# One transfer of 128 rows with a leading dimension of four becomes four transfers of 32 rows

## The chip, the cores and the metric

The kernel runs on one core of a Trainium2 chip. The metric is device time in microseconds (us) of one execution. A core has five engines with their own instruction streams: PE (TensorE, matrix multiplication), DVE (VectorE), ACT (ScalarE), POOL (GpSimd) and SP (SyncE, which here only issues DMAs). 16 DMA engines move data between HBM and the on-chip memories, and are shared by everything that SP and ACT issue.

## The reference, cut to what matters

Two layers, float32 throughout. The first is a recurrent block over x of shape (B=16, L=128, E=512), with H=32 heads of S=16 channels. Its core:

```
r, k, v, w = four projections of a mix of neighbouring time steps, each (b, l, h, s)
def step(s, rkvw):
    r_t, k_t, v_t, w_t = rkvw
    a = k_t[..., :, None] * v_t[..., None, :]      # 16 x 16 for each batch and head
    out = einsum('bhi,bhij->bhj', r_t, u * a + s)
    s = a + w_t[..., :, None] * s
    return s, out
```

It is followed by a group norm, a gate g, a product with Wo, a residual, a layer norm and a feed-forward part with its own gate. The second layer is an attention over each batch of 128 channels by 512 positions against a context: two instance norms, 1x1 convolutions, a softmax of 512 x 512, and a residual.

## The kernel before, in words

The 16 batches are cut into four quarters q of four batches. For each quarter a front computes the projections (streams `a` and `p`) and writes k, v, w, r, g to scratch tensors in HBM (`scr_k` and so on). v is written twice, once of it as `scr_vs`, whose rows are one head of one batch: 16 channels by 128 times, 2,048 floats, 8 KB. Then each batch `bb` goes through the recurrence (stream `scan`), its normalisation (`end`), later the rest of the first layer (`c`, by quarter) and the attention (`l`, `l1`, `l2`, `l3`, by batch). On every engine the instructions of these streams stand in one order that is written out by hand (`ORDER_PE`, `ORDER_POOL`, `ORDER_SP` and so on, lines 32 to 133), as counts of steps of each stream. An engine that waits in one step runs nothing that stands behind it.

The recurrence of a batch has four steps m, one per channel group of the key side. All 128 partitions are used: partition = (channel of k within the group, head), so that every head stands four times, once in each group of 32 partitions. k, w and r come as 128 rows (tiles `KR`, `WG`). v, however, is needed in full by each of the four partition groups: the tile `VB[:, 2 + s]` (s = bb % 2, two buffers) holds the same 32 rows of v four times. It comes with one DMA for each batch, line 499, whose source is the 32 rows with a leading dimension of four and step zero.

For each step POOL computes three products or sums of 128 x 1008 (lines 696, 700, 704) from `KR`, `WG` and this tile. The first of a batch waits on `d_vb` (line 692). DVE runs two scans over their result (line 1150) and multiplies it by r (line 1029), PE sums over the channels (line 1440, semaphore `p_scan`). The products of step k use `VB[:, k % 2]`, so line 696 of step k waits also for PE's line 1440 of step k - 2.

All loads and a part of the stores stand in SP's order. Per batch, stream `load` issues k (484), w (491), v (499), r (505) and then v in the plain layout over the rows of r (510). Each waits for its buffer to be free: the v load of batch bb for POOL's products of batch bb - 2 and for the `scr_vs` stores of the quarter. Between them stand the loads and stores of other streams: `scr_g` stores (422), the copies `LT<-LE` of 32 partitions of the front (453), x (418, 537), the `scr_o` store of the recurrence's result (516), `scr_g` and `scr_o` loads (525, 529), and the context and the output (548, 563). ACT issues the stores of k, v, w and r (786, 788, 831).

Of the kernel before, what the change touches and what calls it, by code (L numbers as in the profile page):

```python
# [6 lines left out]
B, L, E = 16, 128, 512  # L7
NQ = 4
QB = B // NQ
NT = QB * L  # L10
C4 = E // P
H, S = 32, 16
# [236 lines left out]
def rwkv_attention_kernel(nc, x, ctx, w8, w1, w2, td1, td2, wl1, vecs, st01, s0, u, out):  # L249
    with ExitStack() as es:  # L250
        def sb(name, shape):
            return es.enter_context(nc.sbuf_tensor(name, shape, F32))

        def sem(name):
            return es.enter_context(nc.semaphore(name))
# [23 lines left out]
        VB = sb("VB", [P, 4, 2, S, N2])  # L279
# [31 lines left out]
        vs_rows = dr_vs[0:B * H * S * L].rearrange("(q h b n) -> q b h n", q=NQ, h=H, b=QB)  # L311
# [8 lines left out]
        d_vb = [sem(f"d_vb{i}") for i in range(2)]  # L320
# [76 lines left out]
        def stored(n, q):  # L397
            return [(d_st_[n][m], 16 * (q + 1)) for m in range(4)]
# [9 lines left out]
        def of_batch(n, bb):  # L408
            return dr[n][bb // QB].rearrange("c p (b t) -> b p c t", b=QB)[bb % QB]


        def sync_program(sp):
            w = Waits(sp)
# [57 lines left out]
            def stream_load():  # L471
                sp.dma_start(S0[:], s0).then_inc(d_s0, 16)
                yield
                w.wait_ge(d_vec, 32)
                sp.dma_start(dr_vs[0:1].unsqueeze(0), VEC[0:1, 0:1]).then_inc(d_s0, 16)
                yield
                for bb in range(B):
                    q, s = bb // QB, bb % 2
                    for ready in stored("k", q):
                        w.wait_ge(*ready)  # L480
                    if bb >= 2:
                        w.wait_ge(g_kv, 12 * (bb - 1))
                        w.wait_ge(v_kr2, 3 * (bb - 1))
                    sp.dma_start(KR[:, s, 0], of_batch("k", bb)).then_inc(d_kg[s], 16)
                    yield
                    for ready in stored("w", q):
                        w.wait_ge(*ready)
                    if bb >= 2:
                        w.wait_ge(g_kv, 12 * (bb - 1))
                        w.wait_ge(v_kr2, 3 * (bb - 1))  # L490
                    sp.dma_start(WG[:, s], of_batch("w", bb)).then_inc(d_wg[s], 16)
                    yield
                    if bb >= 2:
                        w.wait_ge(g_kv, 12 * (bb - 1))
                    for c in range(C4):
                        w.wait_ge(d_vs[c], 64 * (q + 1))
                    w.wait_ge(d_s0, 32)
                    src = vs_rows[q, bb % QB].unsqueeze(0).to_broadcast([4, H, S * L])
                    sp.dma_start(VB[:, 2 + s].rearrange("p s j n -> p (s j n)"), src).then_inc(d_vb[s], 16)
                    yield  # L500
                    for ready in stored("r", q):
                        w.wait_ge(*ready)
                    if bb >= 2:
                        w.wait_ge(p_end, 3 * bb - 4)
                    sp.dma_start(KR[:, s, 1], of_batch("r", bb)).then_inc(d_rg[s], 16)
                    yield
                    for ready in stored("v", q):
                        w.wait_ge(*ready)
                    w.wait_ge(a_rg, bb + 1)
                    sp.dma_start(KR[:, s, 1], of_batch("v", bb)).then_inc(d_v4, 16)  # L510
                    yield
# [28 lines left out]
            def stream_l(ln):  # L540
# [29 lines left out]
                if ln == 0:  # L570
                    for cs in range(4):
                        w.wait_ge(d_out[cs], 32 * sum(place(bb)[0] == cs for bb in range(B)))
                    yield

            weave(ORDER_SP, {"a": stream_a(), "p": stream_p(), "w": stream_w(), "x": stream_x(), "load": stream_load(), "end": stream_end(), "c": stream_c(),
                             **{n: stream_l(i) for i, n in enumerate(LANES)}})


        def pool_program(po):
            w = Waits(po)  # L580
# [91 lines left out]
            def stream_scan():  # L672
                for k in range(C4 * B):
                    bb, m = divmod(k, C4)
                    bv = VB[:, k % NB]
                    s = bb % 2
                    KO, KE = KR[:, s, 0, m, ODD], WG[:, s, m, ODD]
                    if m == 0:

                        w.wait_ge(d_wg[s], 16 * (bb // 2 + 1))  # L680
                        w.wait_ge(g_id, 3)
                        if bb >= 2:
                            w.wait_ge(a_wr, 4 * (bb - 1))
                        po.tensor_tensor(WP[:, s, :, 1:N2], WG[:, s, :, 0:N2 - 1], WG[:, s, :, N2:L - 1],
                                         ALU.mult).then_inc(g_wp, 1)
                        yield
                        w.wait_ge(d_kg[s], 16 * (bb // 2 + 1))
                        w.wait_ge(g_wp, 2 * bb + 1)
                        po.tensor_tensor(WG[:, s, :, ODD], WG[:, s, :, ODD], KR[:, s, 0, :, EVEN],
                                         ALU.mult).then_inc(g_wp, 1)  # L690
                        yield
                    w.wait_ge(d_vb[s], 16 * (bb // 2 + 1))
                    if k >= NB:
                        w.wait_ge(p_scan, k - NB + 1)
                    vo, ve = bv[:, 0, :, 1:N2], bv[:, 1, :, 1:N2]
                    po.tensor_tensor(vo, KO[:, 0:N2 - 1].unsqueeze(1).to_broadcast([P, S, N2 - 1]),  # L696
                                     VB[:, 2 + s, 0, :, 1:N2], ALU.mult).then_inc(g_kv, 1)
                    yield
                    w.wait_ge(g_wp, 2 * (bb + 1))
                    po.tensor_tensor(ve, KE[:, 0:N2 - 1].unsqueeze(1).to_broadcast([P, S, N2 - 1]),  # L700
                                     VB[:, 2 + s, 1, :, 1:N2], ALU.mult).then_inc(g_kv, 1)
                    yield
                    w.wait_ge(g_kv, 3 * k + 2)
                    po.tensor_tensor(vo, vo, ve, ALU.add).then_inc(g_kv, 1)  # L704
                    yield
# [23 lines left out]
            def stream_l(ln):  # L729
                for k in range(len(BATCHES[ln])):  # L730
                    w.wait_ge(af[ln], 5 * k)
                    yield from mean_rstd(3 + ln, 2, gl_[ln], 4 * k, vf[ln], 4 * (k + 1))

            weave(ORDER_POOL, {"a": stream_a(), "scan": stream_scan(), "end": stream_end(), "c": stream_c(),
                               **{n: stream_l(i) for i, n in enumerate(LANES)}})

# [904 lines left out]
```

## Time and profile before

| | |
|---|---|
| median of 3 runs | 1060.73 us (1055.62 to 1067.09) |
| the profiled execution's own time | 1064.16 us |
| its span in the trace | 1062.4 us |
| PE / DVE / POOL / ACT busy | 85% / 65% / 51% / 37% of the span |
| mean granted TensorE clock | 0.921 |
| DMA | 100.33 MB, mean 94 GB/s |

"Busy" is time with an instruction at work. Idle time is put down to what released the engine at its end. The chain is followed back from the last instruction, at each step to what released it. For a DMA the time from its issue to its landing is given, so it holds the waiting in the DMA queue too.

### The profile page before, as it was taken

Reading aid. Unit: us, or ns where it says so; the run is one execution under the profiler, and the core shown is the slowest. Engines: PE = TensorE matmul, PEld = TensorE weight load, DVE = VectorE, ACT = ScalarE, POOL = GpSimd, SP = SyncE. Lnnn points to the kernel's source line nnn. Section 1 sums busy time; section 2 is a strip of 40 time slices with the busy share of each in tenths; the row PEclk is TensorE's granted clock in tenths of the full one; section 3 lists DMA queues with packets and bytes.
Section 4 is the critical chain, followed back from the end, with each engine's and each line's share of the span. In section 5 each row is a group of like instructions: output and inputs, shape, how many; then the busy total and the mean of one; then the engine's idle time right before and its main releaser. Section 6 shows DMA issues by size and latency. Waiting matters only on the chain.

```text
span 1062.4 us, 10584 instructions
## 1 busy us (share of the span) xinstructions
PE 907.6 (85%) x3588; PEld 400.7 (38%) x3588; DVE 690.3 (65%) x907; ACT 388.9 (37%) x755; POOL 538.6 (51%) x573
## 2 busy tenths in 40 slices
PE   1789969995989958899769988789793999999998
PEld 1234423341334313334324434334341444444454
DVE  5235377764899848899846899569686744362341
ACT  2112212231144112222323544434342354576195
POOL 2000274443769868799658689678677421010100
PEclk9788989898899969699989999899895899999999
DMA  7152455333563535453451322333230123010101
GB/s 258 30 139 73 136 158 119 119 90 99 108 176 123 129 109 121 157 169 105 109 174 37 90 60 64 103 111 98 72 78 22 31 72 116 1 40 1 40 1 39
DMA packets 92983, 100.33 MB, mean 94 GB/s; under 512 B 21890, under 2 KB 63106, under 8 KB 90882
## 3 DMA queue, kind: packets, MB, share of 16 engines
q1 hardware_dynamic: 66306, 78.69, 25.7%
q10 hardware_dynamic: 26624, 20.98, 7.5%
q8 instruction: 28, 0.46, 0.2%
q14 instruction: 25, 0.20, 0.1%
HBM read 65.05 MB, written 33.55 MB: 93 GB/s over the span
## 4 chain that ended last, share of the span: by engine, by line
PE 46%; DMA 22%; POOL 11%; DVE 9%; issue 4%; ACT 4%; ACTq 3%; SPq 2%; POOLq 0%; DVEq 0%
PE PS L1318 30%; DMA VB<-scr_vs 14%; DMA scr_g<-STG 4%; PE PS L1543 3%; POOL VB L704 3%; POOL VB L696 3%; POOL VB L700 3%; PE PS L1325 3%; PE PS L1440 2%; PE PS L1381 2%; ACTq L786 2%; PE PS L1520 2%; DMA KR<-scr_r 2%; DVE VB L1029 2%; DVE VB L1150 1%
## 5 line engine op out<-in xcount | busy, mean ns | idle before, releaser
L1318 PE MATMUL PS<-M,W 128*128 128x512 f32 x672 | 338.4, 646 | 36.8 <-DVE STG L1032 16.6
L696 POOL TENSOR_TENSOR VB<-KR,VB 128x1008 f32<-128x1008 f32 x64 | 127.8, 1997 | 173.2 <-DMA VB<-scr_vs 95.2
L1318 PEld LDWEIGHTS PS<-M,W 128*128 128x128 f32 x672 | 129.8, 205 | 212.0 <-issue 162.6
L1150 DVE TENSOR_TENSOR_SCAN VB<-PS,VB 128x512 f32<-128x512 f32 x128 | 149.2, 1207 | 52.8 <-POOL VB L704 48.5
L704 POOL TENSOR_TENSOR VB<-VB 128x1008 f32<-128x1008 f32 x64 | 151.5, 2367 | 3.5
L1029 DVE TENSOR_TENSOR VB<-VB,PS 128x2048 f32<-128x2048 f32 x64 | 146.0, 2282 | 1.3
L700 POOL TENSOR_TENSOR VB<-WG,VB 128x1008 f32<-128x1008 f32 x64 | 129.2, 2018 | 0.2
L1032 DVE SCALAR_TENSOR_TENSOR PS<-PS,VEC,SX 128x512 f32<-128x512 f32 x80 | 60.2, 753 | 90.9 <-PE PS L1381 81.7
L586 POOL TENSOR_SCALAR NM<-MV 128x2 f32<-128x2 f32 (+1 forms) x24 | 6.6, 273 | 221.9 <-DVE MV L1278 130.0
L1318 PE MATMUL PS<-W,M 128*128 128x512 f32 x224 | 108.4, 610 | 0.0
L1440 PE MATMUL PS<-VB,HEAD 128*32 128x512 f32 x512 | 72.3, 639 | 19.8 <-DVE VB L1029 11.1
L778 ACT ACTIVATE STG<-PS 128x512 f32<-128x512 f32 x48 | 28.5, 594 | 136.9 <-PE PS L1318 117.1
L1296 DVE TENSOR_REDUCE SM<-PS 128x1 f32<-128x512 f32 x64 | 43.8, 688 | 42.3 <-PE PS L1543 42.0
L1381 PE MATMUL PS<-LE,W 32*128 32x512 f32 x64 | 43.1, 758 | 30.0 <-DVE M L1029 11.1
L1318 PE MATMUL PS<-W,SX 128*128 128x512 f32 x128 | 61.2, 597 | 0.0
L1543 PE MATMUL PS<-LS 128*128 128x512 f32 x112 | 60.3, 636 | 0.0
L1318 PEld LDWEIGHTS PS<-W,M 128*128 128x128 f32 x224 | 41.4, 195 | 45.7 <-issue 44.7
L1029 DVE TENSOR_TENSOR M<-PS,EXT 128x512 f32<-128x512 f32 x80 | 55.1, 689 | 2.1
L852 ACT ACTIVATE PS<-WP 128x512 f32<-128x512 f32 x64 | 38.2, 598 | 42.3 <-DVE VB L1150 35.5
L1520 PE MATMUL PS<-LS,WL 128*128 128x512 f32 x56 | 32.6, 679 | 20.1 <-ACT LS L937 15.2
L972 ACT ACTIVATE LE<-PS,SM 128x512 f32<-128x512 f32 x44 | 30.0, 683 | 51.4 <-DVE SM L1296 51.2
L1032 DVE SCALAR_TENSOR_TENSOR STG<-STG,PS 128x512 f32<-128x512 f32 x32 | 21.6, 680 | 36.9 <-ACT STG L776 18.3
(166 smaller groups left out, 1267.7 us busy)
## 6 DMA issues: line engine op xcount, KB each, us to landing
VB<-scr_vs SPq DMA_DIRECT2D x16, 1024.0 KB
W<-in_w SPq DMA_DIRECT2D x8, 1024.0 KB, 9.5
scr_vs<-STG ACTq DMA_DIRECT2D x64, 64.0 KB, 4.2
scr_v<-STG ACTq DMA_DIRECT2D x16, 256.0 KB, 5.2
scr_w<-STG ACTq DMA_DIRECT2D x16, 256.0 KB, 2.0
scr_k<-STG ACTq DMA_DIRECT2D x16, 256.0 KB, 2.0
KR<-scr_k SPq DMA_DIRECT2D x16, 256.0 KB, 4.9
WG<-scr_w SPq DMA_DIRECT2D x16, 256.0 KB, 5.4
```

What stands on the lines that cost most here:

```text
L696: po.tensor_tensor(vo, KO[:, 0:N2 - 1].unsqueeze(1).to_broadcast([P, S, N2 - 1]), VB[:, 2 + s, 0, :, 1:N2], ALU.mult).then_inc(g_kv, 1)
L700: po.tensor_tensor(ve, KE[:, 0:N2 - 1].unsqueeze(1).to_broadcast([P, S, N2 - 1]), VB[:, 2 + s, 1, :, 1:N2], ALU.mult).then_inc(g_kv, 1)
L704: po.tensor_tensor(vo, vo, ve, ALU.add).then_inc(g_kv, 1)
L1029: return dv.tensor_tensor(o, a, b, op)
L1032: return dv.scalar_tensor_tensor(out=o, in0=a, scalar=s, in1=b, op0=op0, op1=op1)
L1150: sc = dv.tensor_tensor_scan(s_, PS[:, 5, :], b_, 0.0, ALU.mult, ALU.add)
L1296: dv.reduce_max(SM[:, cs, tc, 0:1], PS[:, BANK_L[bb, ("sc", tc)], :], AX_X, negate=True).then_inc(vb[ln], 1)
L1318: mm = pe.matmul(o, l, r, start=i == 0, stop=i == 3)
L1381: mm = pe.matmul(PS[:, ns[i], :], W2[DM * g:DM * g + DM, 2 * i + j, :], low_rank(f, i), start=True, stop=True)
L1440: mm = pe.matmul(PS[32 * g:32 * g + 32, 4, :], HEAD[:, m, 0], VB[:, k % NB, :, 4 * g:4 * g + 4].rearrange("p s j n -> p j s n"), start=m = ...
L1520: pe.matmul(PS[:, n, :], WL[:, j, :], X[:, j, :], start=True, stop=True).then_inc(pf[ln], 1)
L1543: pe.matmul(PS[:, n, :], X[:, 2, tc * P:(tc + 1) * P], X[:, 3, :], start=True, stop=True).then_inc(pb[ln], 1)
```

## The change

The one DMA becomes a loop over the four partition groups, each with a source of 32 rows and no broadcast, all on the same queue and semaphore. The semaphore then rises by 64 for each batch, and POOL's wait is scaled to that. Nothing else changes.

```
-                    src = vs_rows[q, bb % QB].unsqueeze(0).to_broadcast([4, H, S * L])
-                    sp.dma_start(VB[:, 2 + s].rearrange("p s j n -> p (s j n)"), src).then_inc(d_vb[s], 16)
+
+                    for c in range(4):
+                        sp.dma_start(VB[H * c:H * c + H, 2 + s].rearrange("p s j n -> p (s j n)"),
+                                     vs_rows[q, bb % QB]).then_inc(d_vb[s], 16)
                     yield
...
-                    w.wait_ge(d_vb[s], 16 * (bb // 2 + 1))
+                    w.wait_ge(d_vb[s], 64 * (bb // 2 + 1))
```

## Rows read from the trace of the kernel before

**Rows 1.** The page: engines over the span, and the granted clock in 40 slices.
```profile
PE 907.6 (85%) x3588; PEld 400.7 (38%) x3588; DVE 690.3 (65%) x907; ACT 388.9 (37%) x755; POOL 538.6 (51%) x573
...
PEclk9788989898899969699989999899895899999999
```
**Rows 2.** The page: the chain that ended last, by line.
```profile
PE PS L1318 30%; DMA VB<-scr_vs 14%; DMA scr_g<-STG 4%; PE PS L1543 3%; POOL VB L704 3%; POOL VB L696 3%; POOL VB L700 3%; PE PS L1325 3%; PE PS L1440 2%; PE PS L1381 2%; ACTq L786 2%; PE PS L1520 2%; DMA KR<-scr_r 2%; DVE VB L1029 2%; DVE VB L1150 1%
```
**Rows 3.** The chain in time: start us, us, what.
```profile
105.31 23.67 DMA VB<-scr_vs
...
147.60 20.18 DMA scr_g<-STG
...
227.84 19.11 DMA KR<-scr_r
...
654.26 19.05 DMA VB<-scr_vs
```
**Rows 4.** DMA issues: KB of each, median us from issue to landing.
```profile
KR<-scr_k SPq DMA_DIRECT2D x16, 256.0 KB, 4.9
...
KR<-scr_r SPq DMA_DIRECT2D x16, 256.0 KB, 12.7
...
XN<-scr_g SPq DMA_DIRECT2D x4, 1024.0 KB, 5.8
...
LT<-LE SPq DMA_DIRECT2D x16, 64.0 KB, 2.0
```
**Rows 5.** Line 453 (`LT<-LE`): landing, least, median and most.
```profile
DMA to landing us min/median/max: 2.0/2.0/20.0
```
**Rows 6.** Stretches: length, busy us of each engine, clock, DMA share, GB/s.
```profile
110.00:112.00 2.00, 2.00 (x12) 1.21 (x10) 0.00 (x0) 0.79 (x2) 0.11 (x1) 1.00 0.93 357
668.00:672.00 4.00, 2.86 (x12) 0.71 (x9) 0.00 (x0) 0.00 (x0) 0.00 (x0) 1.00 0.24 73
784.00:788.00 4.00, 4.00 (x10) 1.44 (x8) 3.66 (x8) 1.15 (x4) 3.78 (x4) 1.00 0.28 70
```
**Rows 7.** Who waited for whom: us in total, times, longest.
```profile
POOL VB L696 <- DMA VB<-scr_vs: 95.2, 8, 22.3
```
**Rows 8.** POOL in time: three of those eight waits, idle us in brackets.
```profile
129.05 2.00 POOL L696 TENSOR_TENSOR VB<-KR,VB 128x1008 f32<-128x1008 f32 x1 [18.95 <-DMA VB<-scr_vs]
...
246.29 2.00 POOL L696 TENSOR_TENSOR VB<-KR,VB 128x1008 f32<-128x1008 f32 x1 [22.28 <-DMA VB<-scr_vs]
...
539.95 2.00 POOL L696 TENSOR_TENSOR VB<-KR,VB 128x1008 f32<-128x1008 f32 x1 [14.18 <-DMA VB<-scr_vs]
```
**Rows 9.** PE in time: idle us before the instruction in brackets.
```profile
248.86 2.07 PE L1318 MATMUL PS<-M,W 128*128 128x512 f32 x2 [9.71 <-DVE STG L1032]
...
380.90 1.19 PE L1381 MATMUL PS<-LE,W 32*128 32x512 f32 x1 [10.04 <-issue]
```
**Rows 10.** Stretches as in rows 6: a load awaited, the middle, the end.
```profile
105.00:129.00 24.00, 24.00 (x74) 11.70 (x74) 9.73 (x12) 8.54 (x14) 1.60 (x3) 1.00 0.49 153
...
100.00:860.00 760.00, 648.28 (x2754) 277.27 (x2753) 573.97 (x684) 252.60 (x497) 513.98 (x494) 0.91 0.37 105
860.00:1062.40 202.40, 194.97 (x658) 95.55 (x658) 75.76 (x161) 116.53 (x225) 16.69 (x51) 1.00 0.14 41
```
**Rows 11.** Seven stretches behind late loads: last one, and the sum.
```profile
796.00:825.00 29.00, 9.41 (x48) 3.61 (x47) 17.67 (x18) 8.09 (x15) 21.75 (x24) 0.56 0.07 22
sum 182.00, PE 112.36 PEld 46.13 DVE 108.17 ACT 43.50 POOL 113.96; mean PE 16.05 PEld 6.59 DVE 15.45 ACT 6.21 POOL 16.28
```
**Rows 12.** Seven stretches with no late load: second one, and the sum.
```profile
300.00:358.00 58.00, 56.37 (x276) 24.07 (x274) 56.11 (x68) 21.80 (x42) 48.56 (x52) 1.00 0.44 141
...
sum 264.00, PE 244.36 PEld 106.08 DVE 236.19 ACT 105.15 POOL 213.79; mean PE 34.91 PEld 15.15 DVE 33.74 ACT 15.02 POOL 30.54
```
**Rows 13.** SP's issues: line 499 (ns min/median/max), and one of line 422.
```profile
L499 SPq DMA_DIRECT2D VB<-scr_vs x16: 524/582/651, 105.3 to 780.5; - x16
...
363.01 12.91 SPq L422 DMA_DIRECT2D scr_g<-STG  x1
```

## The prediction

> **What bounds the kernel now.** I read the page first. PE is busy 85% of the span and no other engine comes near, but its clock digits fall below 9 in many slices [rows 1]: PE is interrupted, and what interrupts it is what a change can win. Then the chain: after the main matmul line its largest piece is the v load, `VB<-scr_vs`, with 14% (some 149 us) [rows 2]. In order of time it stands there in single pieces of about 20 us, the first of them and a later one shown at 23.67 and 19.05 us, and between them other transfers that take equally long, `scr_g` 20.18 and `KR<-scr_r` 19.11 us [rows 3]. A load of 1 MB need not take that long: `XN<-scr_g`, the same size in 128 rows, lands in 5.8 us [rows 4].
>
> The table of DMA issues shows who else pays. `KR<-scr_k` and `KR<-scr_r` move the same 256 KB into the same tile. The first is issued ahead of the v load and lands in 4.9 us, the second is issued right behind it and lands in 12.7 [rows 4]. `LT<-LE` lands in 2.0 us as a rule and in 20.0 at worst [rows 5].
>
> The windows say why. In 668 to 672 us, when little but the v load is under way, the mean busy share of the 16 DMA engines is 0.24 and 73 GB/s are moved; at 784 to 788 it is 0.28 and 70. With 128-row transfers at work it is 0.93 and 357 GB/s [rows 6]. 0.24 x 16 = 3.8: the v load looks like the work of four engines, and everything queued behind it waits for those four. The source's leading dimension is four. By the Trainium skill (DMA: Bandwidth & Descriptors, section "Why a DMA increments its semaphore by 16 and not by 1") a DMA uses at most as many engines as divide its outermost dimension on both sides, so four here and 16 for 32 rows; the share of 0.24 to 0.28 agrees.
>
> **The load, costed.** An engine at work on it moves 73 / 3.8 = 19 GB/s. 16 of them would move 304, so 1,048,576 bytes take 3.4 us. To that I add the landing of a small transfer of 32 partitions, 2.0 us [rows 4], and three more issues of 0.58 us on SP [rows 13] before the last part is even started, 1.7. The sum is 7.1 us against 19.05 [rows 3], **12.0 us less for each load**. The trace has no 256 KB transfer into 32 partitions, so bounds: below, 5.8 us, the same bytes in 128 rows; above, four times the 4.9 us of a 256 KB load one after another plus 1.7, 21.3 us [rows 4, 13]. I take 7.1, since 73 GB/s is this very load's own rate.
>
> A rule of the Trainium skill speaks against splitting by partitions. SBUF — State Buffer (section "Door 1: The DMA port swizzle") says that 32 partitions reach half of the memory's 16 ports, with an asymptote of about 218 GB/s. By that figure 1 MB would take an estimated 4.8 us in place of my 3.4, and the load 8.5; no row here shows a transfer of this shape at size.
>
> **What POOL gains.** It waited for the v load eight times, 95.2 us in all, 22.3 at most [rows 7]. The three waits above 12 us (18.95, 22.28, 14.18) [rows 8] can give back 12.0 each: 95.2 - 6.95 - 10.28 - 2.18 = 75.8 us. That is a cap, because PE must have nothing else to do: while the first load was awaited PE was busy 24.00 of 24.00 us [rows 10], and that work stays.
>
> **What reaches the end.** The last 202.4 us have PE busy for 194.97 at full clock [rows 10], and the first 100 us hold no v load. I leave both as they are and work on the 760 us between, of which PE is idle 760 - 648.3 = 111.7 us [rows 10]. I read PE's own idle times there. Two come straight from the queue behind the load: 10.04 us before line 1381, which wants an `LT<-LE` issued behind the v load of 358 us, and 9.71 us before line 1318, where DVE was held by ACT, and ACT by `KR<-scr_r` [rows 9]. The others follow as late products. They lie in seven stretches (129 to 147, 227 to 247, 358 to 390, 518 to 554, 673 to 694, 754 to 780, 796 to 825 us), 182 us with PE busy for 112.36 [rows 11]: 69.6 of the 111.7 us of idle. Seven stretches without a late load (200 to 227, 300 to 358, 413 to 466, 466 to 489, 580 to 604, 604 to 654, 705 to 734) have 264 us with 244.36 busy, 92.6% [rows 12].
>
> - *Idle.* If the 182 us ran as the others do, they would take 112.36 / 0.926 = 121 us: **61 us less**. It is below POOL's cap of 75.8, as it must be.
> - *Clock.* PE's granted clock fell to 0.56 over 796 to 825 us, in which it was busy 9.41 of 29 us [rows 11], and the middle has a mean of 0.91 against 1.00 at the end [rows 10]. Were the mean to rise to 0.95, the 648.3 us would shrink by 648.3 x (1 - 0.91/0.95) = 27 us. Not all matmuls are on the path: I take half, **14 us**, with bounds 0 and 27.
> - *SP.* Three more issues of 0.582 us for each of 16 batches are 27.9 us on its queue [rows 13]. Queued behind them are r (line 505), the `scr_g` stores and `LT<-LE`; behind those wait ACT (line 859), ACT's copies into STG and PE (line 1381). About half of the loads are awaited by someone, and of what follows less: I charge a third, **9 us** lost, with bounds 0 and 28. One `scr_g` issue was itself held 12.91 us behind a v load [rows 13]; that goes, and I count nothing for it.
> - *The wait.* 64 in place of 16 per batch costs nothing; POOL waits for the last of four.
>
> Sum: 61 + 14 - 9 = 66 us. The profiled execution took 1064.2 us, so 998 on its own scale. It stands 3.4 us above the median of the runs, so **about 995 us**, say 996.
>
> **The rivals.**
> - *The written order keeps most of it.* The order on each engine was fixed with loads of 20 us in it. PE may meet the scan steps no earlier, and only the direct waits vanish: 9.71 + 10.04 [rows 9] = 20 us, 1044 and so 1041. For it: PE's 24.00 of 24.00 us. Against it: PE and DVE ran at 97% each over 300 to 358 us, where loads were on time [rows 12].
> - *PE alone is left.* The middle runs as densely as the end, 194.97 / 202.4 = 96.3%: 648.3 / 0.963 = 673, 87 us less, with the whole clock term 114, less SP's 9: 105 us, so 1064 - 105 - 3 = 956. Against it: DVE is busy 574 of the 760 us [rows 10], and would be at 87% of 655.
> - *No effect.* The four parts run one after another and together take what the one took, plus SP's 9 us: 1061 to 1070. For it is only that the bytes are the same. The Trainium skill has a rule of this kind (DMA: Bandwidth & Descriptors, "Rules for kernel authors": two transfers to disjoint partition halves serialise, use one over 128 partitions). The share of 0.24 [rows 6] speaks against: the engines were mostly unused.
> - *Slower.* A part of 256 KB into 32 partitions lands like `KR<-scr_k`, in 4.9 us, and the parts do not overlap. The load becomes 21.3 us, 2.3 more at each of the eight awaited ones, 18 us, and SP's 9: 1064 + 27 - 3 = 1088. It decides from a part of (19.05 - 1.7) / 4 = 4.3 us on. Against it: 64 KB into 32 partitions land in 2.0 us [rows 4].
>
> **How the numbers follow.** Forecast 0.60 (its own range 965 to 1025, which holds the bounds of the clock and of SP's issues), PE alone 0.13, written order 0.17, no effect 0.05, slower 0.05. Measurement can tell about 1% of this kernel, 1050 to 1071. Faster by over 1%: 0.60 + 0.13 + nearly all of 0.17, 0.89. Within 1%: 0.06. Slower: 0.05. The range 950 to 1043 takes in both neighbours of the forecast and leaves out the tails of each, no effect and slower, under 0.2 together.
>
> **What would show it.** Right: the v parts land within about 7 us of the first issue; `VB<-scr_vs` leaves the chain or falls under 3%; POOL's 95 us of waiting for it fall under 25; `KR<-scr_r` lands near the 4.9 us of `KR<-scr_k`; the most of `LT<-LE` falls from 20.0 towards 5; the DMA share is near 0.9 for short whiles with no plateau at 0.25; PE busy falls by some 14 us through the clock. Wrong: parts over 4 us each, a DMA share that stays at a quarter, or POOL's line 696 waiting for PE's line 1440 as long as it had waited for the load.

## The result and the profile after

The changed kernel takes 991.95 us (988.33 to 997.10, 4 runs) against 1061.2 us (1055.62 to 1067.09, 4 runs) before: a ratio of 0.935, with a 95% interval of 0.928 to 0.942. The forecast was 996 us in a range of 950 to 1043. The profiled executions have spans of 1062.4 and 989.1 us.

The page of the changed kernel, with the engines and the granted clock [rows 1], and the chain that ended last, by engine and by line [rows 2]. The load is now line 500; lines behind it are two higher than before.
```profile
PE 899.4 (91%) x3588; PEld 398.1 (40%) x3588; DVE 691.0 (70%) x907; ACT 389.1 (39%) x755; POOL 540.4 (55%) x573
...
PEclk9797999799879979699999999999998999999999
...
PE 56%; POOL 23%; DVE 9%; issue 5%; ACT 3%; ACTq 2%; DMA 1%; SPq 0%; POOLq 0%; DVEq 0%
PE PS L1320 37%; POOL VB L706 6%; POOL VB L698 5%; POOL VB L702 5%; PE PS L1383 4%; PE PS L1545 3%; PE PS L1327 3%; PE PS L1442 3%; ACTq L788 2%; PE PS L1522 2%; DVE M L1034 2%; DVE PS L1034 2%; DVE M L1031 2%; PE PS L1456 1%; DVE VB L1031 1%
```
`VB<-scr_vs` has left the chain; all DMAs together hold 1% of it. In its place stand PE and POOL's products.

DMA issues of the changed kernel [rows 4], and the landing of line 453, `LT<-LE` [rows 5]:
```profile
VB<-scr_vs SPq DMA_DIRECT2D x64, 256.0 KB, 7.0
...
KR<-scr_k SPq DMA_DIRECT2D x16, 256.0 KB, 4.3
...
KR<-scr_r SPq DMA_DIRECT2D x16, 256.0 KB, 5.7
```
```profile
DMA to landing us min/median/max: 1.9/2.0/4.9
```
`KR<-scr_r`, still issued right behind the v load, lands in 5.7 us where it had taken 12.7, and the worst `LT<-LE` in 4.9 where it was 20.0: the queue behind the load moves.

Who waited for whom [rows 7], and SP and POOL around the load of batch 2 [rows 8]:
```profile
POOL VB L698 <- PE PS L1442: 78.1, 21, 10.6
...
POOL VB L698 <- DMA VB<-scr_vs: 22.3, 3, 11.2
```
```profile
218.26 2.08 SPq L500 DMA_DIRECT2D VB<-scr_vs  x4
```
```profile
226.23 2.00 POOL L698 TENSOR_TENSOR VB<-KR,VB 128x1008 f32<-128x1008 f32 x1 [11.19 <-DMA VB<-scr_vs]
```
From the first issue to POOL's start are 8.0 us, and POOL's waits for v fell from 95.2 to 22.3 us. Its waits for PE's line 1440 (now 1442) did not grow in their place. In the kernel before they were already
```profile
POOL VB L696 <- PE PS L1440: 77.9, 23, 11.6
```

Stretches of the changed kernel: one in which the v load has the DMA engines to itself [rows 6], then the middle and the end [rows 10].
```profile
112.00:114.00 2.00, 2.00 (x10) 1.11 (x9) 0.00 (x0) 1.71 (x3) 0.00 (x0) 1.00 1.05 216
```
```profile
100.00:786.70 686.70, 639.71 (x2755) 275.11 (x2754) 574.81 (x684) 252.87 (x497) 516.27 (x495) 0.94 0.43 116
786.70:989.10 202.40, 194.86 (x658) 95.44 (x657) 75.60 (x161) 116.52 (x225) 16.64 (x51) 1.00 0.15 41
```
The whole time saved lies in the middle: 760 us became 686.7, the end kept its 202.4. PE's idle there (the stretch less PE's busy time) fell from 111.7 to 47.0 us, and its busy time from 648.3 to 639.7, at a mean clock of 0.94 in place of 0.91.

### The profile page after: what moved, and what is told of

It reads as the page before. It is cut to its first block, busy times and chain, and to the rows that moved or that the text cites. A ratio compares the mean times of both kernels' runs of the same rounds, so it can differ in the third digit from the quotient of the medians.

```text
span 989.1 us, 10632 instructions
## 1 busy us (share of the span) xinstructions
PE 899.4 (91%) x3588; PEld 398.1 (40%) x3588; DVE 691.0 (70%) x907; ACT 389.1 (39%) x755; POOL 540.4 (55%) x573
## 4 chain that ended last, share of the span: by engine, by line
PE 56%; POOL 23%; DVE 9%; issue 5%; ACT 3%; ACTq 2%; DMA 1%; SPq 0%; POOLq 0%; DVEq 0%
PE PS L1320 37%; POOL VB L706 6%; POOL VB L698 5%; POOL VB L702 5%; PE PS L1383 4%; PE PS L1545 3%; PE PS L1327 3%; PE PS L1442 3%; ACTq L788 2%; PE PS L1522 2%; DVE M L1034 2%; DVE PS L1034 2%; DVE M L1031 2%; PE PS L1456 1%; DVE VB L1031 1%
## 5 line engine op out<-in xcount | busy, mean ns | idle before, releaser
L1320 PE MATMUL PS<-M,W 128*128 128x512 f32 x672 | 333.2, 638 | 20.6 <-DVE M L1034 12.6
L1320 PEld LDWEIGHTS PS<-M,W 128*128 128x128 f32 x672 | 127.7, 202 | 193.5 <-issue 160.6
L698 POOL TENSOR_TENSOR VB<-KR,VB 128x1008 f32<-128x1008 f32 x64 | 128.4, 2006 | 100.5 <-PE PS L1442 78.1
L1320 PE MATMUL PS<-W,M 128*128 128x512 f32 x224 | 105.6, 596 | 0.0
L1383 PE MATMUL PS<-LE,W 32*128 32x512 f32 x64 | 45.8, 803 | 20.3 <-DVE M L1031 11.3
L1034 DVE SCALAR_TENSOR_TENSOR LS<-PS,WOB,X 128x512 f32<-128x512 f32 x14 | 10.5, 748 | 52.6 <-PE PS L1320 52.6
L1383 PE MATMUL PS<-LT,W 32*128 32x512 f32 x64 | 46.2, 809 | 0.0
```

What stands on the lines that cost most here:

```text
L1034: return dv.scalar_tensor_tensor(out=o, in0=a, scalar=s, in1=b, op0=op0, op1=op1)
L1320: mm = pe.matmul(o, l, r, start=i == 0, stop=i == 3)
L1383: mm = pe.matmul(PS[:, ns[i], :], W2[DM * g:DM * g + DM, 2 * i + j, :], low_rank(f, i), start=True, stop=True)
```

## The experiments

Ratios are to the kernel before on the same chip, with 95% intervals; where the total of one run is set against that of another, the two may come from different chips, and the ratios are the safer comparison. Diffs are against the changed kernel unless it says otherwise, and are cut to the lines that matter (`...`); where the number of transfers changes, POOL's wait is scaled to it.

**The changed kernel again** (no edit), the base of the later runs.

> The changed kernel once more, on the same chip as the next three, as their base. 988 to 997 us, 0.93 to 0.94 of the kernel before.

990.04 us, ratio 0.935 (0.931 to 0.938).

### What sets the pace of the load

**Two transfers of 64 rows.**
```
+                    for c in range(2):
+                        sp.dma_start(VB[64 * c:64 * c + 64, 2 + s]...,
+                                     vs_rows[q, bb % QB].unsqueeze(0).to_broadcast([2, H, S * L]))...
```


> Two transfers of 64 rows, each with a leading dimension of two and step zero. Theory A (the leading dimension sets how many DMA engines work on a transfer): two engines, DMA share near 0.13 while it runs alone, about 20 to 32 us of data time for each load, slower than the kernel before: 1080 to 1180 us. Theory B (it is only that one transfer is cut into parts that overlap): between before and after, 1000 to 1050 us.

1172.6 us, ratio 1.107 (1.102 to 1.112). A stretch in which little but the load runs, and POOL's wait:
```profile
121.00:125.00 4.00, 4.00 (x10) 1.71 (x9) 1.35 (x2) 0.60 (x1) 0.00 (x0) 1.00 0.13 50
```
```profile
POOL VB L698 <- DMA VB<-scr_vs: 192.9, 12, 31.4
```
The share of 0.13 is two of 16 engines, as it was four in [rows 6]. So it is the leading dimension, not the number of parts, that sets how many engines work. A split in two, with a leading dimension of two, makes the kernel 11% slower. Theory A is shown. The pace of one engine is not fixed, though: 50 GB/s over two engines are 25 each, where four had 73 / 3.8 = 19 each. No run shows why.

**One transfer of 128 rows without the leading dimension.** It reads the quarter's 128 rows one after another, so nearly all partitions, in all four groups, get other rows than they should. The source is then one contiguous megabyte, where it had been 32 rows that lie 32 KB apart, read four times. The bytes, the row of 8 KB and the number of rows written are the same.
```
(against the kernel before)
+        vs_all = dr_vs[0:B * H * S * L].rearrange("(q r n) -> q r n", q=NQ, r=P)
+                    sp.dma_start(VB[:, 2 + s]..., vs_all[q]).then_inc(d_vb[s], 16)
```


> One transfer of 128 rows without the leading dimension: it reads the quarter's 128 rows of 8 KB, so the three later partition groups get other rows than they should; as many bytes, one issue. Theory A (leading dimension): all 16 DMA engines, over 300 GB/s, data time 3 to 3.5 us, landing about 6 us after the issue, total 984 to 992 us, no slower than the change. Theory B (the number of rows or bytes of a single transfer is what made it slow): about 16 us of data time and 1050 to 1065 us.

998.43 us, ratio 0.943 (0.938 to 0.948). The load:
```profile
110.00:113.00 3.00, 3.00 (x17) 1.97 (x16) 0.00 (x0) 1.90 (x3) 0.00 (x1) 1.00 1.04 422
```
The load moves at 422 GB/s on all engines, over the 300 that theory A named, so number of rows and bytes had never been the trouble. Its landing was 8.0 us after the issue in the median, not about 6. Its total missed theory A's range by 6 us, on the slow side, which is taken up below.

**Eight transfers of 16 rows**, run twice.
```
+                    for c in range(8):
+                        sp.dma_start(VB[16 * c:16 * c + 16, 2 + s]...,
+                                     vs_rows[q, bb % QB][16 * (c % 2):16 * (c % 2) + 16])...
```


> Eight transfers of 16 rows in place of four of 32. Theory A (the pace of a part is set by how many memory ports its partitions reach, 217 GB/s for 32 rows, so half of it for 16): DMA share near 1 but only about 110 GB/s while the v load runs alone, the eight parts take about 10 us of data time against 5.2, first POOL waits about 5 us longer each, total 1000 to 1012 us. Theory B (the DMA engines were the only limit, 16 rows still use all 16): data time stays near 5 us plus four more issues, total 990 to 998 us.

> The eight transfers of 16 rows once more, now on one chip with the changed kernel. Its load takes longer (7.9 against 5.8 us of data) and it yet took 984 us beside 992. Theory A (a real difference, from where PE's idle time and so its clock falls): 6 to 10 us below the changed kernel again, PE busy about 887 against 899 us. Theory B (the chip or chance): within 3 us of it.

984.19 us, ratio 0.931 (0.927 to 0.934), and 986.10 us, ratio 0.932 (0.928 to 0.936). The pace:
```profile
144.00:148.00 4.00, 2.53 (x8) 0.98 (x8) 1.98 (x4) 0.00 (x0) 4.00 (x3) 1.00 1.07 143
222.00:224.00 2.00, 2.00 (x16) 1.74 (x15) 2.00 (x2) 0.00 (x0) 0.00 (x0) 1.00 0.99 152
```
With all engines busy in all three, the load moves 422 GB/s into 128 partitions, 216 in parts of 32 and 143 to 152 in parts of 16. So the pace goes down with the partitions that a part covers, as theory A said, though 143 is above the 110 it named. The size of a part goes down with them, and the 422 also had a contiguous source, so these runs do not separate the three. Size alone does not hold a part of 256 KB to 216 GB/s: in the changed kernel, while the loads of k and w run (256 KB each, 128 partitions), more is moved:
```profile
106.00:107.00 1.00, 1.00 (x9) 0.64 (x6) 0.84 (x2) 1.00 (x3) 0.00 (x0) 1.00 1.13 339
```
The total, however, lies below both theories' ranges: the slower load gave the same or a slightly better time. The second time it was 4 us under the changed kernel with PE busy 891.9 against 896.3 us, between the two theories. No cost of the four further issues on SP for each batch shows either. Against the changed kernel on one chip (0.935, 0.931 to 0.938) the intervals overlap, so a gain of eight parts over four is not shown.

### Which part of the gain is which

**v early, but the queue blocked.** Behind the four parts goes a transfer with the old source into a scratch tensor, so this kernel also moves 1 MB more per batch.
```
+                    w.wait_ge(d_dum, 16 * bb)
+                    sp.dma_start(dum, vs_rows[q, bb % QB].unsqueeze(0).to_broadcast([4, H, S * L]))...
```


> The changed kernel, and behind the four parts of each load a further transfer with the old source and its leading dimension of four, into a scratch tensor in HBM that nobody reads: v is early, but the queue behind it is held as before. Theory A (most of the gain is v's own arrival at POOL): 1000 to 1020 us, KR<-scr_r landing at 10 to 13 us again. Theory B (most of it is the queue behind the load): 1040 to 1065 us.

1030.59 us, ratio 0.973 (0.968 to 0.978). POOL's waits for v are 22.0 us, as in the changed kernel. The slow landing of `KR<-scr_r` is back, and about half of PE's wait of 10.04 us for `LT<-LE` [rows 9]:
```profile
KR<-scr_r SPq DMA_DIRECT2D x16, 256.0 KB, 13.5
```
```profile
372.93 1.19 PE L1388 MATMUL PS<-LE,W 32*128 32x512 f32 x1 [5.46 <-issue]
```
Neither theory's range held it; it lies between them. The blocked queue costs at most 1030.6 - 992 = 39 us with v on time; at most, because the added traffic is in it.

**v late, but the queue free.** POOL does idle work ahead of the first product of the eight batches that had waited.
```
+                    if m == 0:
+                        for _ in range(DELAY.get(bb, 0)):      # {0: 23, 2: 25, 5: 26, 9: 26, ...}, 163 in all
+                            w.wait_ge(g_dum, len(done_))
+                            (po.memset(DUM[:], 0.0) if not done_ else
+                             po.tensor_tensor(DUM[:], DUM[:], DUM[:], ALU.mult)).then_inc(g_dum, 1)
...
```


> The changed kernel with idle work on POOL (163 small products of 128 x 128, about 73 us together) ahead of the first product of the eight batches whose load POOL had waited for before: v is late for POOL again, but the DMA queue is free. Theory A (v's arrival and the blocked queue each carry a part of the gain that adds up with the 28 us which the opposite experiment left): 1020 to 1035 us. Theory B (the queue is all that mattered): 990 to 1005 us.

1059.04 us, ratio 1.002 (0.999 to 1.005). The idle work on POOL, the landing of r behind the load, and POOL's first product of batch 2:
```profile
L703 POOL TENSOR_TENSOR DUM<-DUM 128x128 f32<-128x128 f32 x162 | 68.9, 425 | 25.7 <-DMA VB<-scr_vs 13.5
```
```profile
KR<-scr_r SPq DMA_DIRECT2D x16, 256.0 KB, 4.1
```
```profile
248.11 2.00 POOL L708 TENSOR_TENSOR VB<-KR,VB 128x1008 f32<-128x1008 f32 x1
```
All of the gain is gone, with the queue free (`KR<-scr_r` lands in 4.1 us). The idle work stands behind what is left of the wait for v (13.5 us, and 8.1 before the memset), so it holds POOL for 68.9 + 21.6 = 90.5 us, against 95.2 of waits before. That product starts at 248.11 us where it had started at 246.29 [rows 8]: v is as late as it was. DVE's busy time, 688.8 us against 691.0 in the changed kernel, shows no cost of the idle work to DVE.

Both theories fall, and with them the thought that the two causes add up. Against the kernel before, freeing the queue while v stays late brings nothing (1059 us), v early behind a queue still blocked brings 28 (1031), and both together bring 69 (992). They lie on the same stretches. The delay stands in place of the waits only roughly, and this is the limit of the reading.

**The slow load, issued sooner.** The kernel before with two steps of SP's order moved.
```
(against the kernel before, in ORDER_SP)
-    ... load:2 x:1 load:2 a:1 load:1 ...          load:2 end:1 load:2 a:3 ...
+    ... load:3 x:1 load:1 a:1 load:1 ...          load:3 end:1 load:1 a:3 ...
```


> The kernel before, one transfer with the leading dimension of four, with the two steps of SP's order moved (v of batch 0 ahead of x, v of batch 2 ahead of the scr_o store). Theory A (a slow load can be partly hidden by issuing it sooner): POOL's 22.3 us wait in batch 2 goes, 1035 to 1052 us. Theory B (what stands behind the load pays for it): within 1% of the kernel before.

1043.83 us, ratio 0.987 (0.982 to 0.992). POOL's wait:
```profile
POOL VB L697 <- DMA VB<-scr_vs: 70.9, 7, 16.6
```
As theory A had it: the 22.3 us wait of batch 2 is gone, and a fifth of the gain could be had without touching the transfer.

### What a still earlier load brings

**The same order in the changed kernel.**
```
-    ... load:2 x:1 load:2 ...      load:2 end:1 load:2 a:3 ...
+    ... load:3 x:1 load:1 ...      load:3 end:1 load:1 a:3 ...
```

> The changed kernel with two steps of SP's order moved: the v load of batch 0 ahead of the x load, and that of batch 2 ahead of the scr_o store which it stood behind. Theory A (what is left of POOL's wait for v is SP's order, 8.7 and 11.2 of its 22.3 us): that wait falls from 22.3 to under 10 us, and the total by 5 to 12 us against the changed kernel. Theory B (PE or DVE carry the path there): the wait falls and the total stays within 3 us.

994.46 us, ratio 0.939 (0.935 to 0.943). POOL's waits for v fell as expected, to 5.3 us, 4.0 of them in batch 0, and the total did not:
```profile
114.67 2.00 POOL L699 TENSOR_TENSOR VB<-KR,VB 128x1008 f32<-128x1008 f32 x1 [4.00 <-DMA VB<-scr_vs]
```
```profile
POOL VB L699 <- PE PS L1443: 95.7, 22, 18.3
```
Part of the wait turned into one for PE: 95.7 us where it had been 78.1. That is theory B's account. The total came 4.4 us above the changed kernel's 990.04 and not within its 3, with intervals that overlap. DVE in time, first in the changed kernel, then here, then in the run with one transfer of 128 rows:
```profile
118.58 3.81 DVE L1034 SCALAR_TENSOR_TENSOR M<-SX,VEC,EXT 128x512 f32<-128x512 f32 x3
```
```profile
120.72 7.50 DVE L1035 SCALAR_TENSOR_TENSOR M<-SX,VEC,EXT 128x512 f32<-128x512 f32 x3
```
```profile
119.71 7.50 DVE L1034 SCALAR_TENSOR_TENSOR M<-SX,VEC,EXT 128x512 f32<-128x512 f32 x3
```
In both runs the earlier v of batch 0 makes three steps of DVE take 7.50 us in place of 3.81, and DVE's busy time goes from 691.0 to 698.3 and 697.8. The next runs ask what that is. It fits the few us that both totals are over, but no run takes it away in these two kernels.

**A quarter of the load.** From batch 2 on, three partition groups keep the v of batches 0 and 1.
```
+                    for c in range(4 if bb < 2 else 1):
...
+                    w.wait_ge(d_vb[s], 64 + 16 * (bb // 2))
```


> From batch 2 on only the first of the four parts is loaded, the three other partition groups keep the v of batches 0 and 1, so a quarter of the bytes and of the issues. Theory A (the load is off the path after the change, and what is left of it is worth little): within 6 us of the changed kernel. Theory B (the load's remaining 5 to 8 us and its issues on SP still cost): 12 to 25 us below it.

1003.64 us, ratio 0.948 (0.943 to 0.953): **slower** than with all four parts, and outside both theories. DVE was busy 703.4 us against 692.2 in the changed kernel run again. DVE in time, first in the changed kernel run again, then here, and POOL here:
```profile
219.02 2.74 DVE L1034 SCALAR_TENSOR_TENSOR M<-SX,VEC,EXT 128x512 f32<-128x512 f32 x4
```
```profile
225.19 8.28 DVE L1034 SCALAR_TENSOR_TENSOR M<-SX,VEC,EXT 128x512 f32<-128x512 f32 x4
```
```profile
225.58 2.22 POOL L698 TENSOR_TENSOR VB<-KR,VB 128x1008 f32<-128x1008 f32 x1 [7.00 <-DMA VB<-scr_vs]
227.76 2.44 POOL L702 TENSOR_TENSOR VB<-WG,VB 128x1008 f32<-128x1008 f32 x1
230.28 2.65 POOL L706 TENSOR_TENSOR VB<-VB 128x1008 f32<-128x1008 f32 x1
```
The same four steps of DVE, with two inputs (`SX`, `EXT`) from the on-chip memory SBUF, take 2.74 us where POOL waits for v, and 8.28 us where POOL's products run beside them. The early v had set POOL to work just then.

**The same, with POOL held back there.**
```
+HOLD = {0: ("v_m1", 8), 2: ("v_m1", 12), 9: ("v_kr", 8)}
+                    if m == 0 and bb in HOLD:
+                        w.wait_ge(...)      # until DVE's steps of that place are done
```


> The kernel with one part loaded from batch 2 on (three partition groups keep older v; 1003.6 us), plus three waits on POOL: its first product of batches 0, 2 and 9 also waits until DVE's elementwise steps M<-SX,VEC,EXT of that place are done. Theory A (a load that comes early makes POOL's products run into those steps, and DVE is held): the steps at 225 and 501 us take 2.7 and 5.5 us again in place of 8.3 and 11.9, DVE busy falls from 703 to about 692, and the total falls to 988 to 998 us although POOL waits longer. Theory B (other causes): 1003 us or, with POOL's waits added, more.

991.60 us, ratio 0.938 (0.935 to 0.942): 12 us faster than without the waits, intervals apart. DVE's steps and its busy time, and what POOL waited for:
```profile
225.91 2.74 DVE L1037 SCALAR_TENSOR_TENSOR M<-SX,VEC,EXT 128x512 f32<-128x512 f32 x4
```
```profile
PE 896.2 (91%) x3588; PEld 397.3 (40%) x3588; DVE 687.6 (69%) x907; ACT 388.7 (39%) x755; POOL 537.9 (54%) x573
```
```profile
POOL VB L701 <- DVE M L1037: 26.0, 3, 13.1
```
POOL waits 26 us for DVE, and the kernel is faster for it. So the collision was the cost, shown by taking it away. No difference to the changed kernel can be measured any more: three quarters of the load, taken away, bring no time.

**The same waits in the changed kernel.**

> The changed kernel with the same three waits on POOL. Theory A: the steps at 491 us take 5.5 in place of 8.1 us, those at 117 us 2.7 in place of 4.4; the total is 983 to 989 us, a little under the 990 of the changed kernel. Theory B: 990 us or some us more, since POOL starts later.

992.24 us, ratio 0.938 (0.934 to 0.942): theory B, no gain. DVE is busy 687.6 us here too, against 691.0 and 692.2 in the two runs of the changed kernel, so the collisions there were short, some 4 us in all. That POOL's later start takes back what they gave is argued, not shown.

No version was shown to be faster than the change itself.

## Why the prediction was right, and where it was off

- **Four engines.** Right, and shown: a leading dimension of four gave a DMA share of 0.24, of two 0.13, and with 128, 32 or 16 rows outermost it was 1.04, 1.05 and 1.07.
- **The load, 7.1 us.** It took 8.0. The data term was mis-sized: I took 19 GB/s on each of 16 engines, 304 in all. That is no fixed pace of an engine: it was 216 / 16 = 13.5 here, 25 with a leading dimension of two, and 26 with 128 rows. The busy share is full but the pace is 216 GB/s, so 4.9 us and not 3.4. The rule of the Trainium skill that I had set beside it (SBUF — State Buffer, "Door 1: The DMA port swizzle": 32 partitions reach half of the ports, about 218 GB/s) is the better one: the trace agrees with 216, and with its 8.5 us for the load. For partitions 0 to 15 the table of that section gives about 109 GB/s. The run with parts of 16 moved 143 to 152; those windows hold several queued parts that go to different partitions, and no run times a lone one.
- **The Trainium skill's rule against splitting** (DMA: Bandwidth & Descriptors, "Rules for kernel authors"), named for the rival "no effect" with 0.05, does not carry here. It compares parts with one transfer over all engines. Where that one had only four, four parts win: 0.935 of the time.
- **POOL's gain**, capped at 75.8 us: its wait for v fell by 72.9.
- **PE's idle, 61 us less:** it fell by 64.7. Behind that stands the right way of asking: not how long the load is on the chain (149 us), but how dense PE is where no load is late.
- **The clock, 14 us:** PE's busy time in the middle fell by 8.6, with a mean granted clock of 0.94 where I had supposed 0.95.
- **SP's issues, 9 us lost:** no loss shows. Eight parts in place of four issue four more per batch and were no slower, and one part in place of four, once held off DVE, was no faster. This term failed. The sum was 61 + 14 - 9 = 66, and the profiled executions differ by 64.7 + 8.6 = 73.3 us: the 9 us are more than the difference. The clock term was too large by 5 and the idle term too small by 4; that the sum comes so near owes something to luck.
- **The signs of being wrong:** I had named POOL's line 696 waiting for PE's line 1440 as long as it had waited for the load, and did not say that it did so already. It waited 77.9 us before and 78.1 after, so the waits for v (95.2 us) went and were not exchanged.
- **The neighbours of the forecast:** 47.0 us of PE's idle are left in the middle, so "PE alone is left" (956 us) did not come, and a still earlier load brings nothing (994 and 1004 us). The written order did not keep the gain. That rival gave 20 us to the direct waits alone; with the queue free and v late the run shows nothing for them.
- **v or queue.** I had told the two direct waits of PE and the late products apart as if each had its own us. They share them: v late costs the whole 69 us with the queue free, the blocked queue at most 39 with v on time, and both together 69. The forecast did not rest on it, as it took the seven stretches whole.

## What to carry to other kernels

A DMA share that stays at a small fraction (here 4/16 and 2/16) while one transfer runs says that it works on a few engines; look at its outermost dimension, for all that is queued behind it pays too. Four transfers with 32 rows outermost beat one with a leading four. Once a load is in time, making it earlier can cost: what it releases may run into another engine's work.

## What the runs showed of the hardware that was not expected

- At full busy share the load moved 422 GB/s in one transfer into 128 partitions, 216 in parts of 32 and 143 to 152 in parts of 16, all in rows of 8 KB. The busy share does not show the difference. Size of the part and layout of the source changed too, as said above.
- A `SCALAR_TENSOR_TENSOR` of 128 x 512 on DVE with two inputs from SBUF takes 0.69 us by itself (2.74 for four), and 2.07 on average (8.28 for four) beside POOL products of 128 x 1008, of which that of line 702 itself grows from 2.00 to 2.44 us. The Trainium skill says so (SBUF — State Buffer, "Who interferes with whom": a DVE instruction with two SBUF inputs contends with a GpSimd operation that reads SBUF, and one waits for the other); the trace agrees.
